# GpSimd makes the edges' one-hot rows, and the landmark loop's products and block copies are dealt out anew

## The chip, the cores and the metric

One core of a Trainium2 chip runs the whole program in one launch. The metric is the device time in microseconds, the median of several executions. For the kernel before they are 2507.85, 2507.54 and 2505.82 us, the median 2507.54.

## The reference, cut to what matters

The program is a "macaron" block over 32 x 256 rows of 128 values: an int8-quantised product, a Nystrom attention with a graph part, the quantised product again, a mixture of eight experts, a small attention, and the experts again, each behind a layer norm and added to the rows. The change touches two pieces of the first attention:

```python
# edges: 16384 of them, rows and columns in 0..1023, values drawn
contrib = adj_vals * data[adj_rows, adj_cols]
A_raw = jax.ops.segment_sum(contrib, adj_rows, num_segments=n)   # n = 256 here
# landmarks: means of 8 rows of q and k, 8 heads of 64, 32 landmarks, 32 batches
q_l = q.reshape(b, h, m, l, dh).mean(axis=3)
k_l = k.reshape(b, h, m, l, dh).mean(axis=3)
attn2 = jax.nn.softmax(jnp.einsum('bhid,bhjd->bhij', q_l, k_l), axis=-1)
attn2_inv = moore_penrose_pinv(attn2, 6)   # scale: max row sum times max column sum over everything
```

The kernel turns the edge list into a dense 256 x 256 matrix `Wadj`, whose product with the scores is summed along its rows.

## The kernel before, in words

Everything is written by hand: each engine has one instruction stream, and semaphores order them. `S[name]` is a semaphore, `wait_ge` waits for its value, `then_inc` raises it, `hold` is a wait with a count behind it.

**The group steps** (about 30 to 284 us of the profile). The rows are worked in eight groups of 1024 (`NG` = 8): layer norm (L332 to L362), quantised product (L413 to L438, L446 on GpSimd, L455 and L465 on TensorE), layer norm again, and the landmark means (L483 on VectorE, L489 on TensorE). Between these pieces each engine has a share of the edges, 16 tiles of 128 edges a group (`EG` = 16, 128 tiles in all). For one tile VectorE makes three rows of 256 bf16 values for each of the 128 edges: `EK` (L1708, one at the edge's column), `ER` (L1710, one at the edge's row) and `EV[0]` (L1712, the high part of the value at the column). ScalarE makes `EV[1]` and `EV[2]` out of EK and the value's two lower parts (L1721, two a tile). TensorE adds six products of 128x256 to PSUM (L1433), ER as the stationary side, EV as the moving one. Eight slots (`DEEP`) are in use; a slot is free when the products of the tile eight before are done (`ed_mm`). The order in which tiles and the other pieces follow one another is written out by hand in `first_dve`, `first_act` and `first_pe`; GpSimd has only `q_pool` (L446) once a group and `early_pool` (L1414 in the first group, L1417 in the sixth). `early_pe` puts parts of batch 0's attention (L1381 to L1393) between the products of groups 1 to 5.

**The landmark loop** (284 to 316 us) has four passes c, one for each pair of heads. In `b_pe` TensorE makes the pair's keys of all landmarks (L1458, into `H[2:4]`), then its queries (L1466, into `H[0:2]`), then 16 small products of query and key landmarks (L1476, into `TRq` and `Yq`; 32 records). VectorE copies the keys out (`KL`, L1757, L1758), ScalarE the queries (`QL`, L1618, L1619); there is one buffer of each, so both wait for the pass's small products. Then VectorE copies four 32x256 blocks out of TRq (L1763) and ScalarE four out of Yq (L1622) to `S2`. VectorE waits for all eight, takes the row maximum (L1736) and subtracts it (L1737); ScalarE takes the exponential (L1625); VectorE sums, inverts and multiplies (L1741 to L1743, `normal`) one pass later. After the loop the column sums of the four passes are made by TensorE (L1482) and their maxima by VectorE (`column`, L1751); `total` (L1747) takes the row sums. GpSimd makes the largest of them over all partitions (L1677), which scales the start of the inverse. SP moves blocks of S2 to `XB` (L2485) as soon as a pass is normalised, XB is transposed (L1504) and copied (L1627); then six passes of the inverse follow (L1558 to L1577).

After that the rounds run until 2514 us: experts (L876, L908), small attention, routing. The change has nothing in them.

Of the kernel before, what the change touches and what calls it, by code (L numbers as in the profile page):

```python
# [8 lines left out]
ALU = mybir.AluOpType  # L9
# [17 lines left out]
DEEP = 8  # L27
# [64 lines left out]
def build(nc, ins, out):  # L92
    ctx = ExitStack()
    with ctx:
# [1331 lines left out]
        def edges_pe(pe, g, lo, hi):  # L1426
            for j in range(lo, hi):
                q = j % DEEP
                pe.wait_ge(S["ed_v"], 3 * EG * g + 3 * (j + 1))
                pe.wait_ge(S["ed_a"], 2 * EG * g + 2 * (j + 1))  # L1430
                for u in range(2):
                    for k in range(3):
                        mm = pe.matmul(H[:, u, 0:SEQ], ER[:, q, u * P:(u + 1) * P], EV[:, q, k, :],  # L1433
                                       start=False, stop=False)
                mm.then_inc(S["ed_mm"], 1)
# [16 lines left out]
        def b_pe(pe):  # L1452
            pe.wait_ge(S["lm_cp"], LEAD + NG)
            for c in range(4):
# [5 lines left out]
                mm.then_inc(S["b_l"], 1)  # L1460
                if c >= 1:
# [6 lines left out]
                mm.then_inc(S["b_l"], 1)  # L1468
                pe.wait_ge(S["b_ql"], c + 1)
                pe.wait_ge(S["b_kl"], c + 1)  # L1470
                if c >= 1:
                    pe.wait_ge(S["b_s2d"], 4 * c)
                    pe.wait_ge(S["b_s2a"], 4 * c)
# [13 lines left out]
            pe.wait_ge(S["b_s2a"], 16)  # L1487
# [5 lines left out]
            pe.wait_ge(S["b_s2d"], 16)  # L1493
# [119 lines left out]
        def b_act(act):  # L1613
            for c in range(4):
# [5 lines left out]
                act.wait_ge(S["b_s"], c + 1)  # L1620
                for i in range(4):
# [80 lines left out]
        def edges_dve(dve, g, lo, hi):  # L1702

            for j in range(lo, hi):
# [5 lines left out]
                dve.tensor_scalar(ER[:, q, :], iota, erf[:, bass.ds(col, 1)], None,  # L1710
                                  ALU.is_equal).then_inc(S["ed_v"], 1)
                dve.tensor_scalar(EV[:, q, 0, :], iota, ecf[:, bass.ds(col, 1)], evh[:, bass.ds(col, 1)],  # L1712
                                  ALU.is_equal, ALU.mult).then_inc(S["ed_v"], 1)

        def edges_act(act, g, lo, hi):

            for j in range(lo, hi):
                q = j % DEEP
                hold(act, S["ed_v"], 3 * EG * g + 3 * j + 1)
# [4 lines left out]
        def b_dve(dve):  # L1724
# [8 lines left out]
            def shift(c):  # L1733
                dve.wait_ge(S["b_s2a"], 4 * (c + 1))
                dve.wait_ge(S["b_s2d"], 4 * (c + 1))
# [17 lines left out]
            for c in range(4):  # L1753
# [8 lines left out]
                for i in range(4):  # L1762
# [3 lines left out]
                if c >= 1:  # L1766
                    total(c - 1)
            column(0)
            column(1)
            normal(3)  # L1770
# [720 lines left out]
        def _(pool):  # L2491
# [60 lines left out]
            for p in range(2):  # L2552
# [9 lines left out]
                             tmp[:, 2, :].rearrange("p (g d) -> p d g", g=AH)).then_inc(S["w_pm"], 1)  # L2562
            for g in range(NG):
                q_pool(pool, g, FIRST_Q)
                early_pool(pool, g)
            b_pool(pool)
# [179 lines left out]
```

## Time and profile before

| | |
|---|---|
| median of three executions | 2507.54 us |
| the profiled execution, timed | 2515.66 us |
| its span, first to last instruction | 2513.9 us |
| TensorE products, weight loads | 2036.8 us, 1594.7 us busy |
| VectorE, ScalarE, GpSimd | 1426.1, 1236.0, 648.7 us busy |
| mean granted TensorE clock | 0.909 |

The page gives busy times, the chain of work that ended last (followed back from the last instruction), and groups of instructions by line, with the idle time of the engine before them and who ended it. A timeline row has start, duration, engine, line, operation, what it writes and reads with shapes, and the count merged into the row; in brackets stands the engine's idle time before it and the releaser as the profile infers it. A merged row's duration runs to the end of its last instruction. DVE is VectorE, ACT is ScalarE, POOL is GpSimd, PE and PEld are TensorE's products and weight loads. Float products of 32 bits show two records each.

### The profile page before, as it was taken

To read this page: it belongs to the slowest core of one execution; us is meant where nothing else is said; L and a number is where in the kernel's file an instruction comes from. 1 tells how busy PE (TensorE), PEld (TensorE's weight loads), DVE (VectorE), ACT (ScalarE), POOL (GpSimd) and SP (SyncE) were. 2 spreads that over 40 slices of the span, in tenths; PEclk is the share of its full clock that TensorE was granted. 3 is DMA by queue.
4 is the path that set the end of the run, shared out by engine and by line. 5 is a ranking of instruction groups with operands and counts; after the bars stand their busy time and mean duration, and the time that the engine had idled before them with its cause. 6 is when DMAs were issued, how large, how long until landed. Compare 5 with 4: busy or idle time off the path is not lost.

```text
span 2513.9 us, 38918 instructions
## 1 busy us (share of the span) xinstructions
PE 2036.8 (81%) x13610; PEld 1594.7 (63%) x13610; DVE 1426.1 (57%) x4130; ACT 1236.0 (49%) x2670; POOL 648.7 (26%) x663
## 2 busy tenths in 40 slices
PE   2766773587878888998899889989998999788884
PEld 1555552476557556875787578757875886665764
DVE  5877536453556675566556565666566356356522
ACT  3766413444446455555555564555455446335431
POOL 3111003333131133124223322332233124013052
PEclk9777885699889899999899999999999999899997
DMA  7100000112211211312132213221322312312121
GB/s 237 43 1 1 1 1 0 31 45 64 56 47 44 65 52 57 85 55 55 52 91 57 65 39 89 62 65 32 92 67 60 88 52 68 89 29 61 41 62 47
DMA packets 228948, 141.29 MB, mean 56 GB/s; under 512 B 116489, under 2 KB 206732, under 8 KB 228754
## 3 DMA queue, kind: packets, MB, share of 16 engines
q1 hardware_dynamic: 174320, 85.60, 13.4%
q0 software_dynamic: 16960, 34.74, 4.6%
q10 hardware_dynamic: 37474, 18.46, 2.6%
q8 instruction: 110, 1.80, 0.3%
q14 instruction: 84, 0.69, 0.1%
HBM read 82.48 MB, written 57.16 MB: 56 GB/s over the span
## 4 chain that ended last, share of the span: by engine, by line
PE 53%; DVE 24%; ACT 12%; issue 6%; DMA 2%; POOL 2%; SPq 1%; ACTq 0%; POOLq 0%; DVEq 0%
PE PS L908 17%; PE PS L876 9%; DVE AR L1085 3%; PE PS L1207 3%; PE PS L1170 3%; PE PS L1188 3%; PE PS L1433 2%; PE PS L1193 2%; ACT AR L1141 2%; DVE small L332 2%; ACT AR L837 2%; ACT AR L362 2%; DVE AR L795 2%; DVE xnT L1269 1%; PE PS L911 1%
## 5 line engine op out<-in xcount | busy, mean ns | idle before, releaser
L908 PE MATMUL PS<-AR,W 128*128 128x256 f32 x2560 | 653.0, 404 | 20.9 <-DVE AR L795 15.0
L795 DVE TENSOR_TENSOR AR<-AR,PS 128x512 f32<-128x512 f32 (+1 forms) x384 | 228.6, 597 | 653.9 <-ACT AR L837 525.8
L908 PEld LDWEIGHTS PS<-AR,W 128*128 128x128 f32 x2560 | 499.8, 204 | 92.1 <-issue 17.0
L837 ACT ACTIVATE AR<-PS 128x512 f32<-128x512 f32 (+1 forms) x384 | 201.1, 525 | 556.5 <-PE PS L908 439.1
L1085 DVE TENSOR_REDUCE AR<-PS 128x2 f32<-128x512 f32 x512 | 337.2, 688 | 160.0 <-PE PS L1170 155.6
L1141 ACT ACTIVATE AR<-PS 128x512 f32<-128x512 f32 x512 | 303.6, 600 | 236.3 <-PE PS L1193 231.9
L876 PE MATMUL PS<-AR,WO 128*128 128x256 f32 (+1 forms) x1536 | 357.7, 383 | 0.0
L876 PEld LDWEIGHTS PS<-AR,WO 128*128 128x128 f32 (+1 forms) x1536 | 295.5, 193 | 42.8
L1170 PE MATMUL PS<-AR 128*128 128x256 bf16 x1024 | 204.8, 287 | 40.4 <-DVE AR L1085 25.9
L743 POOL DMA_INDIRECT AR<-YE,gidx1c x128 | 128.8, 1007 | 379.8 <-issue 231.4
L743 POOL DMA_INDIRECT AR<-YE,gidx x128 | 128.3, 1002 | 350.9 <-ACT AR L1141 310.8
L1188 PE MATMUL PS<-AR 128*128 128x256 bf16 x1024 | 204.5, 282 | 13.3 <-ACT AR L1141 11.2
L726 POOL DMA_INDIRECT XE<-AR,sidx x128 | 130.6, 1020 | 274.8 <-DVE AR L795 142.8
L1193 PE MATMUL PS<-AR,pick 128*128 128x256 bf16 x1024 | 201.1, 279 | 0.0
L1433 PE MATMUL PS<-AR 128*128 128x256 bf16 x768 | 127.3, 333 | 81.6 <-ACT AR L1721 35.0
L726 POOL DMA_INDIRECT XE<-xn,sidx x128 | 126.8, 991 | 225.1 <-ACT AR L1141 135.7
L1170 PEld LDWEIGHTS PS<-AR 128*128 128x128 bf16 x1024 | 99.4, 119 | 103.7 <-DVE AR L1085 55.1
L1433 PEld LDWEIGHTS PS<-AR 128*128 128x128 bf16 x768 | 87.5, 118 | 116.9 <-DVE AR L1712 58.1
L1207 PE MATMUL PS<-AR 128*32 128x256 f32 x2048 | 141.6, 395 | 8.1 <-ACT AR L1141 8.1
L1188 PEld LDWEIGHTS PS<-AR 128*128 128x128 bf16 x1024 | 103.6, 117 | 49.7 <-ACT AR L1141 42.5
L1721 ACT ACTIVATE AR<-AR 128x256 bf16<-128x256 bf16 x256 | 107.5, 496 | 19.8 <-DVE AR L1708 17.0
L362 ACT ACTIVATE AR<-X,small 128x128 f32<-128x128 f32 x248 | 102.3, 489 | 13.6 <-DVE small L347 13.1
(359 smaller groups left out, 2771.5 us busy)
## 6 DMA issues: line engine op xcount, KB each, us to landing
AR<-XE SPq DMA_DIRECT2D x128, 128.0 KB, 2.1
YE<-AR ACTq DMA_DIRECT2D x128, 128.0 KB
AR<-QD SPq DMA_DIRECT2D x384, 32.0 KB
QD<-AR SPq DMA_DIRECT2D x8, 768.0 KB, 5.2
AR<-KD SPq DMA_DIRECT2D x64, 96.0 KB
W<-in_L_ffn_w_kernel_dram SPq DMA_DIRECT2D x2, 2560.0 KB, 13.5
OD<-AR SPq DMA_DIRECT2D x128, 36.0 KB
X<-in_L_attn_dense_dram SPq DMA_DIRECT2D x8, 512.0 KB, 4.5
```

What stands on the lines that cost most here:

```text
L726: pool.indirect_dma_start(rows_of(p, g), bass.IndirectOffsetOnAxis(ap=sidx[tab][:, k, t:t + 1], axis=0), rows[:, t, :], None, bounds_check ...
L743: pool.indirect_dma_start(yg[:, k, t, :], None, results_of(p, g), bass.IndirectOffsetOnAxis(ap=at[:, k, t:t + 1], axis=0), bounds_check=E ...
L795: ins = dve.tensor_tensor(hf[:, cols], gl[i % 2][:, cols], H[:, 2 * (i % 2) + 1, cols], ALU.mult)
L837: ins = act.activation(gl[i % 2][:, cols], H[:, 2 * (i % 2), cols], ACT.Gelu_apprx_tanh)
L876: mm = pe.matmul(Y[:, 0, 0:CAP], WO[rows, e, b, :], hid[e % 2][rows, b, :], start=(b == 0), stop=(b == HBLK - 1))
L908: mm = pe.matmul(H[:, b0, b * CAP:(b + 1) * CAP], w0[:, e, hb * P:(hb + 1) * P], xeT[e % 2], start=True, stop=True)
L1085: dve.tensor_reduce(mx[c % 2][:, :, b], score_bank(c, b).rearrange("p (h q) -> p h q", h=2), AX.X, ALU.max).then_inc(S["a_mx"], 1)
L1141: act.activation(EX[:, li, :], H[:, 2 + i % 2, :], ACT.Exp, scale=A_SCALE).then_inc(S["a_ex"], 1)
L1170: mm = pe.matmul(score_bank(c, b)[:, h * 256:(h + 1) * 256], keys(c, P, h, b), queries(c, b), start=True, stop=True)
L1188: pe.matmul(o[:, h * 256:(h + 1) * 256], keys(c, P, h, b), queries(c, b), start=(h == 0), stop=False, skip_group_check=True)
L1193: mm = pe.matmul(o.rearrange("p (h q t) -> p q h t", h=2, q=2)[:, q], pick[:, q * PB + b:q * PB + b + 1].broadcast_to([P, P]), MP[c % 2].r ...
L1433: mm = pe.matmul(H[:, u, 0:SEQ], ER[:, q, u * P:(u + 1) * P], EV[:, q, k, :], start=False, stop=False)
```

## The change

The row ER is made by GpSimd, in a new function `edges_pool`, with a semaphore of its own (`ed_r`); its 16 tiles a group are put around `q_pool` and `early_pool`. TensorE waits for `ed_r` too, and VectorE's count `ed_v` goes up by two a tile. In `b_pe` the key products of pass c+1 are issued between the query products and the small products of pass c. Of the eight block copies of a pass VectorE makes two and ScalarE six. After the loop `normal(3)` stands ahead of `column(0)` and `column(1)`.

```diff
@@ -1426,7 +1426,8 @@
         def edges_pe(pe, g, lo, hi):
             for j in range(lo, hi):
                 q = j % DEEP
-                pe.wait_ge(S["ed_v"], 3 * EG * g + 3 * (j + 1))
+                pe.wait_ge(S["ed_v"], 2 * EG * g + 2 * (j + 1))
+                pe.wait_ge(S["ed_r"], EG * g + j + 1)
                 pe.wait_ge(S["ed_a"], 2 * EG * g + 2 * (j + 1))
                 for u in range(2):
                     for k in range(3):
@@ -1451,13 +1452,17 @@
 
         def b_pe(pe):
             pe.wait_ge(S["lm_cp"], LEAD + NG)
-            for c in range(4):
+
+            def landmark_keys(c):
                 if c >= 1:
                     pe.wait_ge(S["b_kl"], c)
                 for a in range(2):
                     mm = pe.matmul(H[:, 2 + a, :], wqkv[:, 512 + c * P:512 + (c + 1) * P],
                                    mT[:, a * 512:(a + 1) * 512], start=True, stop=True)
                 mm.then_inc(S["b_l"], 1)
+
+            landmark_keys(0)
+            for c in range(4):
                 if c >= 1:
                     pe.wait_ge(S["b_ql"], c)
                 else:
@@ -1466,11 +1471,13 @@
                     mm = pe.matmul(H[:, a, :], wqkv[:, c * P:(c + 1) * P], mT[:, a * 512:(a + 1) * 512],
                                    start=True, stop=True)
                 mm.then_inc(S["b_l"], 1)
+                if c < 3:
+                    landmark_keys(c + 1)
                 pe.wait_ge(S["b_ql"], c + 1)
                 pe.wait_ge(S["b_kl"], c + 1)
                 if c >= 1:
-                    pe.wait_ge(S["b_s2d"], 4 * c)
-                    pe.wait_ge(S["b_s2a"], 4 * c)
+                    pe.wait_ge(S["b_s2d"], 2 * c)
+                    pe.wait_ge(S["b_s2a"], 6 * c)
                 for q in range(8):
                     for j in range(2):
                         mm = pe.matmul((TRq, Yq)[j][:, q, :], QL[64 * j:64 * j + 64, q * P:(q + 1) * P],
@@ -1484,13 +1491,13 @@
 
             for a in range(3):
                 column(a)
-            pe.wait_ge(S["b_s2a"], 16)
+            pe.wait_ge(S["b_s2a"], 24)
             for c in range(4):
                 for j in range(2):
                     mm = pe.matmul(Y[32 * c:32 * c + 32, j, 0:SEQ], ql0[64 * j:64 * j + 64, c, :],
                                    kT0[64 * j:64 * j + 64, c, :], start=True, stop=True, skip_group_check=True)
             mm.then_inc(B("a3")[0], 1)
-            pe.wait_ge(S["b_s2d"], 16)
+            pe.wait_ge(S["b_s2d"], 8)
             for u in range(2):
                 for c in range(4):
                     for j in range(2):
@@ -1618,6 +1625,9 @@
                 act.mul(QL, flat2(H[:, 0:2, :]), DH ** -0.5)
                 act.mul(ql0[:, c, :], H[:, 0, 0:LM], DH ** -0.5).then_inc(S["b_ql"], 1)
                 act.wait_ge(S["b_s"], c + 1)
+                for i in range(2, 4):
+                    act.copy(S2[32 * i:32 * i + 32, 2 * c, :, :],
+                             TRq[32 * i:32 * i + 32, :, 32 * i:32 * i + 32]).then_inc(S["b_s2a"], 1)
                 for i in range(4):
                     act.copy(S2[32 * i:32 * i + 32, 2 * c + 1, :, :],
                              Yq[32 * i:32 * i + 32, :, 32 * i:32 * i + 32]).then_inc(S["b_s2a"], 1)
@@ -1707,16 +1717,21 @@
                 col = EG * g + j
                 dve.tensor_scalar(EK[:, q, :], iota, ecf[:, bass.ds(col, 1)], None,
                                   ALU.is_equal).then_inc(S["ed_v"], 1)
-                dve.tensor_scalar(ER[:, q, :], iota, erf[:, bass.ds(col, 1)], None,
-                                  ALU.is_equal).then_inc(S["ed_v"], 1)
                 dve.tensor_scalar(EV[:, q, 0, :], iota, ecf[:, bass.ds(col, 1)], evh[:, bass.ds(col, 1)],
                                   ALU.is_equal, ALU.mult).then_inc(S["ed_v"], 1)
 
+        def edges_pool(pool, g, lo, hi):
+
+            for j in range(lo, hi):
+                hold(pool, S["ed_mm"], EG * g + j + 1)
+                pool.tensor_scalar(ER[:, j % DEEP, :], iota, erf[:, bass.ds(EG * g + j, 1)], None,
+                                   ALU.is_equal).then_inc(S["ed_r"], 1)
+
         def edges_act(act, g, lo, hi):
 
             for j in range(lo, hi):
                 q = j % DEEP
-                hold(act, S["ed_v"], 3 * EG * g + 3 * j + 1)
+                hold(act, S["ed_v"], 2 * EG * g + 2 * j + 1)
                 for k, v in ((1, evm), (2, evl)):
                     act.activation(EV[:, q, k, :], EK[:, q, :], ACT.Copy,
                                    scale=v[:, bass.ds(EG * g + j, 1)]).then_inc(S["ed_a"], 1)
@@ -1731,8 +1746,8 @@
                 return v[:, 16 * c:16 * c + 16]
 
             def shift(c):
-                dve.wait_ge(S["b_s2a"], 4 * (c + 1))
-                dve.wait_ge(S["b_s2d"], 4 * (c + 1))
+                dve.wait_ge(S["b_s2a"], 6 * (c + 1))
+                dve.wait_ge(S["b_s2d"], 2 * (c + 1))
                 ch.link(dve.tensor_reduce(of(mx2, c), seg(c), AX.X, ALU.max))
                 dve.tensor_tensor(seg(c), seg(c), bc(of(mx2, c), 16, LM), ALU.subtract).then_inc(S["b_sh"], 1)
 
@@ -1759,15 +1774,15 @@
                 if c >= 1:
                     normal(c - 1)
                 dve.wait_ge(S["b_s"], c + 1)
-                for i in range(4):
+                for i in range(2):
                     dve.tensor_copy(S2[32 * i:32 * i + 32, 2 * c, :, :],
                                     TRq[32 * i:32 * i + 32, :, 32 * i:32 * i + 32]).then_inc(S["b_s2d"], 1)
                 shift(c)
                 if c >= 1:
                     total(c - 1)
+            normal(3)
             column(0)
             column(1)
-            normal(3)
             column(2)
             total(3)
             column(3)
@@ -2560,9 +2575,13 @@
 
             pool.tensor_copy(tmp[:, 7, :].rearrange("p (d g) -> p d g", g=AH),
                              tmp[:, 2, :].rearrange("p (g d) -> p d g", g=AH)).then_inc(S["w_pm"], 1)
+            pool.wait_ge(S["ed_prep"], 1)
             for g in range(NG):
+                edges_pool(pool, g, 0, 4)
                 q_pool(pool, g, FIRST_Q)
+                edges_pool(pool, g, 4, 12)
                 early_pool(pool, g)
+                edges_pool(pool, g, 12, EG)
             b_pool(pool)
             round_pool(pool)
 
```

## Rows read from the trace of the kernel before

**Rows 1.** The page's chain that ended last, share of the span by engine.

```profile
PE 53%; DVE 24%; ACT 12%; issue 6%; DMA 2%; POOL 2%; SPq 1%; ACTq 0%; POOLq 0%; DVEq 0%
```

**Rows 2.** Windows by stage: length, busy PE, PEld, DVE, ACT, POOL, granted clock, DMA.

```profile
30.00:284.00 254.00, 169.61 (x1103) 127.56 (x1104) 188.86 (x786) 165.30 (x406) 33.05 (x10) 0.78 0.15 45
...
284.00:303.40 19.40, 14.88 (x89) 7.88 (x89) 12.69 (x24) 8.78 (x17) 0.68 (x2) 1.00 0.01 1
```

**Rows 3.** Groups by line and shape, 0 to 620 us: busy us, mean ns, idle.

```profile
L1721 ACT ACTIVATE AR<-AR 128x256 bf16<-128x256 bf16 x256 | 107.5, 496 | 19.8 <-DVE AR L1708 17.0 <-DVE AR L1710 2.6
...
L446 POOL TENSOR_SCALAR xnT<-tmp 128x1024 bf16<-128x1024 f32 x8 | 29.6, 3696 | 162.0 <-DVE tmp L417 162.0
```

**Rows 4.** Timeline of ScalarE in the fifth group, from the root on.

```profile
154.28 0.30 ACT L356 ACTIVATE small<-small,epsc 128x8 f32<-128x8 f32 x1 [1.23 <-DVE small L342]
...
156.00 0.91 ACT L1721 ACTIVATE AR<-AR 128x256 bf16<-128x256 bf16 x2 [0.51 <-DVE AR L1710]
...
156.81 3.17 ACT L362 ACTIVATE AR<-X,small 128x128 f32<-128x128 f32 x8
...
159.89 3.28 ACT L1721 ACTIVATE AR<-AR 128x256 bf16<-128x256 bf16 x8
```

**Rows 5.** Timeline of TensorE in the fifth group, tile 2 and early products.

```profile
160.92 1.44 PE L1433 MATMUL PS<-AR 128*128 128x256 bf16 x6 [2.12 <-DVE AR L1710]
...
164.40 3.26 PE L1389 MATMUL PS<-AR 128*128 128x512 f32 x4
```

**Rows 6.** Timeline of VectorE and GpSimd where both work.

```profile
152.11 3.67 POOL L446 TENSOR_SCALAR xnT<-tmp 128x1024 bf16<-128x1024 f32 x1 [27.08 <-DVE tmp L417]
...
153.51 0.17 DVE L337 TENSOR_TENSOR small<-small 128x8 f32<-128x8 f32 x1
...
154.36 0.28 DVE L1710 TENSOR_SCALAR AR<-AR 128x256 bf16<-128x256 bf16 x1
...
154.56 0.34 DVE L1712 TENSOR_SCALAR AR<-AR 128x256 bf16<-128x256 bf16 x1
...
154.81 1.05 DVE L1708 TENSOR_SCALAR AR<-AR 128x256 bf16<-128x256 bf16 x1
...
170.39 1.23 DVE L438 TENSOR_TENSOR X<-X,tmp 128x1024 f32<-128x1024 f32 x1
...
199.87 2.35 POOL L1417 TENSOR_TENSOR AR<-AR,wvb 128x1024 f32<-128x1024 f32 x1 [13.06 <-ACT AR L1406]
...
201.28 2.02 DVE L438 TENSOR_TENSOR X<-X,tmp 128x1024 f32<-128x1024 f32 x1
```

**Rows 7.** Windows of TensorE: length, busy, clock, around a long gap.

```profile
171.20:175.50 4.30, 0.00 (x0) 0.81 0.00 0
...
175.50:184.00 8.50, 6.49 (x30) 0.50 0.00 1
```

**Rows 8.** Timeline of the landmark passes c = 0 to 2.

```profile
288.70 2.06 PE L1476 MATMUL PS<-AR 64*128 64x128 f32 x32 [1.20 <-ACT AR L1619]
...
295.27 0.18 DVE L1758 COPY AR<-PS 128x32 f32<-128x32 f32 x1
...
295.95 2.06 PE L1476 MATMUL PS<-AR 64*128 64x128 f32 x32 [1.56 <-ACT AR L1619]
...
297.94 1.98 PE L1458 MATMUL PS<-AR 128*128 128x512 f32 x4
...
298.06 1.53 ACT L1622 COPY AR<-PS 32x256 f32<-32x256 f32 x4 [2.15 <-PE PS L1476]
...
298.06 1.77 DVE L1763 COPY AR<-PS 32x256 f32<-32x256 f32 x4 [1.00 <-PE PS L1476]
...
303.11 0.18 DVE L1758 COPY AR<-PS 128x32 f32<-128x32 f32 x1
...
303.39 2.06 PE L1476 MATMUL PS<-AR 64*128 64x128 f32 x32 [1.75 <-ACT AR L1619]
```

**Rows 9.** Timeline: GpSimd's reduction ahead of the inverse.

```profile
322.29 0.35 POOL L1677 PARTITION_ALL_REDUCE AR<-AR  x1 [31.62 <-DVE AR L1776]
```

## The prediction, made blind

> **What bounds the kernel now.** I read the chain that ended last first [rows 1]: the products of the later rounds (L908, L876) carry it, and the change does not touch them. Its whole text lies in two stretches ahead of the rounds, so I asked for these as windows [rows 2]: the eight group steps with the edges (30 to 284 us), and the start of the landmark stage. In the first no engine is full (TensorE 170 of 254 us, VectorE 189, ScalarE 165, GpSimd 33) and the granted clock is 0.78 of full; in the second it is full. So the question in both is which wait ends last, and I took the timeline of one group step (150 to 182 us; six of the eight look alike) and of one landmark pass.
>
> In the group step ScalarE's root of the next layer norm stands idle 1.23 us for VectorE's statistics, and later 0.51 us for an edge row of VectorE [rows 4]. Then come eight normalised rows (3.17 us) and edge tile 2 (0.91 us a tile for its two rows), and TensorE's product of tile 2 starts at 160.92 after 2.12 us of idle time [rows 4, 5]: the view names L1710, but ScalarE's tile 2 started at 159.89, so it is ScalarE that comes last. Behind that product follow turn, products, update, statistics, root: the loop that sets the step's length. In the landmark pass the loop is: small products L1476, block copies, maximum, subtraction, exponential, QL, next L1476.
>
> **Part 1: 128 edge rows ER leave VectorE.** Each costs VectorE 0.20 us from start to start (154.36 to 154.56 in [rows 6]), 1.6 us in the eight tiles between the statistics and the next root, 3.2 us a group. It is worth only what stands still for it. At the root it is at most the 1.23 us, beside it the 0.51 us, and TensorE's gap bounds both: tile 2 can't start before the landmark copy is out, its EK made, and ScalarE's 0.91 us done, about 1.4 us before 160.92. Working the six groups through in the same manner gives 0.2, 1.0, 1.2, 1.65, 1.8 and 2.25 us (the last three with a smaller gap at tile 0 too), together 8.1 us; first and last group nothing. A second gain could follow: behind the 2.1 us gap TensorE went to half clock and the four 512-column products took 3.26 us [rows 5], where the same shape takes 1.98 at full clock [rows 8]. A shorter gap may spare that, 1.3 to 2 us in up to three groups, so 6 us. The edge stage gains between 0 and 14 us if nothing else changes.
>
> **GpSimd's price.** The trace has no such row there. Nearest is L446, 3.70 us for 1024 columns with two operations [rows 3], so 0.9 us for 256; sixteen make 15 us and L446 3.7, in a step of 31: GpSimd keeps up. It runs eight slots ahead of TensorE, whose own new wait so costs nothing by this count; queued behind GpSimd's waits is L446, which may start under 1 us later than now, but its readers come 6 us after its end. The cover goes if an ER takes over 1.6 us.
>
> **What it does to VectorE** decides this part. During L446 (152.11 to 155.78) three edge rows pass at 0.28 to 0.34 us, and the fourth takes 1.05 instead of 0.28 [rows 6]; all eight L446 show one such stall of 0.77 us. And the update L438, 1.23 us alone, takes 2.02 beside GpSimd's L1417 [rows 6]. So two engines do stop each other in pieces of about 0.8 us, not for a whole instruction. An ER of 0.9 us may hold VectorE for 0 to 0.77 us. Placing the sixteen by the products that free their slots: ER 13 to 15 fall on the update, two on tiles 8 to 15, one or two on L417 and on tiles 2 to 5. Bounds: no stall, or 0.77 us on the update in eight groups (6 us) with the 8 us gain gone and up to 1 us a group behind tiles 2 to 5: +14 us. I take the middle, as the one L446 row stalls about a fifth of its length: half of the 8.1 lost (gain 4), 0.39 x 8 = 3.1 on the update, 1 us of clock won: **-1.9 us, bounds -14 and +14**.
>
> A rule bears on this. In the Trainium skill, page SBUF — State Buffer, section Who interferes with whom, the shared port pair is a lock held by whichever started first for its whole instruction, against VectorE operations in a two-port mode or with two SBUF inputs. The trace agrees on the kind (L1708, L438), not on the length: L337, with two SBUF inputs, took its usual 0.17 us inside L446, and three edge rows passed [rows 6]. By that rule a tile would cost VectorE much more; it is the third rival.
>
> **Part 2: key products ahead of the small ones.** TensorE now does key(c+1) between query(c) and small(c). Four records at 0.43 us make 1.73 us ([rows 8], L1458: 1.98 with the tail). It waits for VectorE's KL copy, which small(c) needs too, so for c = 1 and 2 it simply goes between. c = 0: TensorE is free at 287.50 (288.70 less 1.20), key(1) ends 289.25 instead of 288.70: +0.55. c = 1: the KL copies end 295.45, key(2) ends 297.2 instead of 295.95: +1.25. c = 2: 303.29, so 305.05 instead of 303.39: +1.65. c = 3 has none. What it takes away, key before the next query, was done while VectorE and ScalarE worked, and nobody waited for it: gain 0. Sum **+3.5 us**.
>
> **Part 3: block copies 4+4 become 2+6.** Both engines start together; four take VectorE 1.77 us, ScalarE 1.53 [rows 8]. Six on ScalarE take 0.36 + 5 x 0.39 = 2.3 us, and the maximum waits for all: +0.54 each, four times **+2.2 us**. VectorE's two saved copies only lengthen its wait. The table load of the first exponential stays under it.
>
> **Part 4: normal(3) before two column maxima.** The XB rows leave 1.2 us sooner, but the inverse's start also waits for GpSimd's reduction at 322.29 [rows 9], which follows all of VectorE's maxima and sums; these are the same work in another order, with 0.1 us less idle: **-0.1 us**.
>
> **The clock in part 2 and 3.** TensorE's gaps in this loop are now 1.2 to 1.75 us and the clock stays full [rows 2, 8]. After the change they are 3.4 to 4.1 us (from the end of query(c+1), 1.7 us after small(c), to the next KL copy, 5.8 us after it). In the edge stage gaps of 4.3 us end at half clock: 171.2 to 175.5 averages 0.81, then 0.50 for 8.5 us [rows 7]; from 80 us on the stage has seven gaps of over 4 us, and each ends or is followed at once by half clock. If it falls here, key and small (1.73 + 2.06) double twice, small once more: bounds 0 and +9.7. I take **+4**, since a fall late in the gap doubles only part. The inverse behind already runs its first two passes at half clock; it may gain or lose one pass, about 2 us, left in the range.
>
> Sum: -1.9 + 3.5 + 2.2 - 0.1 + 4.0 = **+7.7 us**. The profiled execution spans 2513.9 us (2515.66 timed), so its like would span 2521.6. It is 8 us above the median of the runs; I carry the difference over: 2507.5 + 7.7 = **2515.2 us**.
>
> **Rivals.** *A, ends faster:* GpSimd's ER meets VectorE hardly ever or for a few tenths, and the shorter gaps keep TensorE's clock up in the edge stage. Price -14, landmark +5.6 with no fall: -8.4, 2499 us. It decides when the edge stage wins over 10.6 us. For it: sixteen short rows against VectorE's idle 6 us plus 3.2 a step. Against: it needs all gains at once. *B, no change:* edge stage about -2, the landmark passes longer but at full clock: +3.7, 2511 us. *C, lock for the whole ER:* 0.92 instead of 0.39 on the update (7.4 us), no gain at the root, 1 to 2 rows behind tiles 2 to 5 (7 us), with +9.6 in the landmark stage: +24, 2532 us. Against: the rows that passed inside L446. *D, the change doesn't do what it says:* ER could be late for TensorE if GpSimd needs over 1.6 us; then each tile follows GpSimd, far above C. I leave it under C.
>
> **Chances and range.** Forecast 0.37, B 0.27, A 0.23, C (with D) 0.13. About 0.2% (5 us) is what a measurement of this kernel can tell from no change: slower 0.50, same 0.27, faster 0.23. The likeliest case alone has 2510 to 2520. The range reaches through A's price by 1 us, and into C until under 2 in 10 are out: 2498 to 2528.
>
> **What would show it.** In the landmark stage small products start 8.5 to 9.5 us apart instead of 7.3 to 7.4, with a key product right ahead; ScalarE has six copies of about 2.3 us. The granted clock of 290 to 320 tells the 4 us. In the edge stage: L1708's rows with a mean above 0.31 us or L438 above 1.3 speak for contention; ScalarE's idle before its root should vanish; GpSimd's row should be 0.5 to 1.0 us. I am wrong if the small products come no later, or if the edge stage shrinks by over 10 us.

## The result, and the profile after

The kernel before took 2508.9 us (median of 22 runs), the changed one 2518.7 us (22 runs). The ratio is 1.0043, with a 95% interval of 1.0029 to 1.0057: slower by about 10 us, 0.4%. The forecast was +7.7 us, the median of before carried with it 2515.2 us, the range 2498 to 2528.

The page of after, its first line, the busy time of each engine and the chain that ended last (before's shares are [rows 1]):

```profile
span 2526.2 us, 39046 instructions
...
PE 2043.0 (81%) x13610; PEld 1596.7 (63%) x13610; DVE 1407.3 (56%) x3994; ACT 1237.8 (49%) x2678; POOL 773.6 (31%) x791
...
PE 51%; DVE 23%; ACT 12%; issue 6%; DMA 3%; POOL 2%; SPq 1%; ACTq 0%; POOLq 0%; DVEq 0%
```

The page alone tells little: GpSimd's work has grown, the chain is the same. The places have to be read. First the landmark stage, which answers to [rows 8]. Timeline of after: start, duration, engine, line, operation, tiles, count, and in brackets the idle time before it. L1460 is the key product, L1483 the small one, L1629 and L1632 are ScalarE's copies, L1778 VectorE's.

```profile
295.56 2.06 PE L1483 MATMUL PS<-AR 64*128 64x128 f32 x32
...
302.81 3.35 PE L1460 MATMUL PS<-AR 128*128 128x512 f32 x4 [3.28 <-DVE AR L1773]
306.09 2.33 PE L1483 MATMUL PS<-AR 64*128 64x128 f32 x32
308.47 0.75 ACT L1629 COPY AR<-PS 32x256 f32<-32x256 f32 x2 [5.27 <-PE PS L1483]
308.47 0.86 DVE L1778 COPY AR<-PS 32x256 f32<-32x256 f32 x2 [4.11 <-PE PS L1483]
309.25 1.52 ACT L1632 COPY AR<-PS 32x256 f32<-32x256 f32 x4
310.81 0.69 DVE L1751 TENSOR_REDUCE AR<-AR 128x16 f32<-128x512 f32 x1 [1.47 <-ACT AR L1632]
...
314.22 3.78 PE L1460 MATMUL PS<-AR 128*128 128x512 f32 x4 [3.89 <-DVE AR L1773]
317.93 3.19 PE L1483 MATMUL PS<-AR 64*128 64x128 f32 x32
...
326.97 3.63 PE L1483 MATMUL PS<-AR 64*128 64x128 f32 x32 [3.93 <-DVE AR L1773]
```

Small products start 10.53, 11.84 and 9.04 us apart; before, 7.25 and 7.44, and the prediction had 8.5 to 9.5. In each of the middle passes a key product of 3.4 to 3.8 us stands right ahead of the small one, where the same shape took 1.98 us [rows 8]. VectorE is done with its two copies at 309.33 and stands 1.47 us for ScalarE's six. The windows of the same stretch (length, busy PE, PEld, DVE, ACT, POOL, granted clock, DMA share) show where the long records come from:

```profile
290.20:302.80 12.60, 9.32 (x48) 4.69 (x48) 5.48 (x10) 5.91 (x11) 0.68 (x2) 1.00 0.00 0
302.80:321.20 18.40, 14.50 (x77) 8.10 (x78) 7.18 (x14) 4.35 (x12) 0.00 (x0) 0.72 0.01 2
321.20:330.60 9.40, 5.47 (x37) 3.97 (x37) 5.64 (x10) 3.90 (x9) 0.00 (x0) 0.82 0.01 1
```

Up to 302.80 the clock is at its upper level, 2.4 GHz; behind the gap of 3.28 us it has fallen towards the lower one, 1.2 GHz.

Now the edge stage. Groups by line and shape of after, 30 to 285 us: busy us, mean ns of one, idle before them. L1718 is EK, L1720 EV, L337 the first statistics row.

```profile
L1720 DVE TENSOR_SCALAR AR<-AR 128x256 bf16<-128x256 bf16 x128 | 51.0, 399 | 0.0
L1718 DVE TENSOR_SCALAR AR<-AR 128x256 bf16<-128x256 bf16 x128 | 38.2, 299 | 1.2
...
L417 DVE TENSOR_SCALAR tmp<-AR,small 128x128 f32<-128x128 f32 x64 | 14.7, 304 | 0.3
L438 DVE TENSOR_TENSOR X<-X,tmp 128x1024 f32<-128x1024 f32 x8 | 12.0, 1497 | 0.3
...
L337 DVE TENSOR_TENSOR small<-small 128x8 f32<-128x8 f32 x15 | 6.1, 409 | 0.5
```

and the same view of before:

```profile
L1712 DVE TENSOR_SCALAR AR<-AR 128x256 bf16<-128x256 bf16 x128 | 45.6, 356 | 0.0
...
L417 DVE TENSOR_SCALAR tmp<-AR,small 128x128 f32<-128x128 f32 x64 | 13.3, 282 | 0.3
L438 DVE TENSOR_TENSOR X<-X,tmp 128x1024 f32<-128x1024 f32 x8 | 10.6, 1325 | 0.3
```

VectorE has 39.9 us of rows less, and of the kinds that are left several take longer: EV by 43 ns, L417 by 22, L438 by 172, L337 by 237 (172 before); EK does not (310 before). GpSimd's own row, which the trace of before did not have, has a mean of 0.99 us (0 to 620 us):

```profile
L1727 POOL TENSOR_SCALAR AR<-AR 128x256 bf16<-128x256 bf16 x128 | 125.5, 993 | 81.5 <-PE PS L1434 71.1 <-DVEq L1710 8.9
```

It stands 71.1 of its 81.5 idle us for slots that TensorE frees: GpSimd keeps up.

**Milestones.** I cut every trace at three instructions: the copy of the last group's landmark product (L483), behind which the landmark stage begins, GpSimd's reduction [rows 9] and VectorE's first quantising maximum (L413) of the rounds. Starts in us, and the length of the two stretches between:

| kernel | L483 | reduction | first L413 | landmark | inverse |
|---|---|---|---|---|---|
| before | 283.46 | 322.29 | 400.62 | 38.83 | 78.33 |
| after | 289.87 | 340.41 | 423.48 | 50.54 | 83.07 |
| landmark part only | 287.69 | 338.24 | 421.25 | 50.55 | 83.01 |
| edge part only | 285.19 | 323.95 | 402.25 | 38.76 | 78.30 |
| edge part again | 285.17 | 323.94 | 402.22 | 38.77 | 78.28 |
| keys only | 288.89 | 335.82 | 414.17 | 46.93 | 78.35 |
| copies only | 288.73 | 332.09 | 410.31 | 43.36 | 78.22 |
| after, gap filled | 287.17 | 331.56 | 414.26 | 44.39 | 82.70 |
| edges, own rows | 279.31 | 318.80 | 397.00 | 39.49 | 78.20 |
| before, own rows | 287.92 | 326.66 | 409.37 | 38.74 | 82.71 |
| before, idle GpSimd rows | 293.15 | 331.87 | 410.14 | 38.72 | 78.27 |
| two buffers | 287.74 | 322.14 | 404.84 | 34.40 | 82.70 |
| normal(3) first | 289.18 | 327.99 | 406.34 | 38.81 | 78.35 |
| both mended | 278.59 | 312.94 | 391.19 | 34.35 | 78.25 |

The landmark stretch repeats within 0.1 us with before's passes (38.72 to 38.83 in six traces; the seventh, edges with own rows, had 39.49, at a clock of 0.95 in its last 27 us where before has 0.97: its last two column products took 1.89 us, in the six 1.13 to 1.25), so there one trace decides a difference of a few us. The edge stage does not: with unchanged edge code it ended at 283.46, 287.69, 287.74, 288.73, 288.89 and 289.18, and with only L413's wait changed at 287.92; the mean of these seven is 287.7. The 6.4 us between before's and after's L483 are therefore mostly an early trace of before: with GpSimd's rows and the old wait of L413 the ends are 285.17, 285.19, 287.17 and 289.87, mean 286.9. And what follows, from L413 to the end of the span, took 2095 to 2113 us on the first chip, with the same code in all; a single profile says nothing on it.

The first chip ran before, after, and the two halves and two single edits of the first experiments. All other kernels ran on two other chips, where the kernel before itself took 2586 and 2590 us; each ratio below is to runs of before on the same chip.

### The profile page after: what moved, and what is told of

The parts are those of the page before. It is cut to its first block, busy times and chain, and to the rows that moved or that the text cites. A ratio compares the mean times of both kernels' runs of the same rounds, so it can differ in the third digit from the quotient of the medians.

```text
span 2526.2 us, 39046 instructions
## 1 busy us (share of the span) xinstructions
PE 2043.0 (81%) x13610; PEld 1596.7 (63%) x13610; DVE 1407.3 (56%) x3994; ACT 1237.8 (49%) x2678; POOL 773.6 (31%) x791
## 4 chain that ended last, share of the span: by engine, by line
PE 51%; DVE 23%; ACT 12%; issue 6%; DMA 3%; POOL 2%; SPq 1%; ACTq 0%; POOLq 0%; DVEq 0%
PE PS L908 16%; PE PS L876 8%; PE PS L1207 3%; DVE AR L1085 3%; PE PS L1170 3%; PE PS L1188 3%; PE PS L1193 2%; ACT AR L1141 2%; DVE small L332 2%; PE PS L1434 2%; ACT AR L362 2%; ACT AR L837 2%; DVE xnT L1269 1%; PE PS L911 1%; DVE AR L795 1%
## 5 line engine op out<-in xcount | busy, mean ns | idle before, releaser
L908 PE MATMUL PS<-AR,W 128*128 128x256 f32 x2560 | 642.4, 398 | 19.6 <-DVE AR L795 15.0
L908 PEld LDWEIGHTS PS<-AR,W 128*128 128x128 f32 x2560 | 490.6, 201 | 88.8 <-issue 17.0
L1188 PE MATMUL PS<-AR 128*128 128x256 bf16 x1024 | 204.3, 282 | 13.6 <-ACT AR L1141 11.4
L1727 POOL TENSOR_SCALAR AR<-AR 128x256 bf16<-128x256 bf16 x128 | 125.5, 993 | 81.5 <-PE PS L1434 71.1
```

The lines of the kernel that those rows point to most:

```text
L908: mm = pe.matmul(H[:, b0, b * CAP:(b + 1) * CAP], w0[:, e, hb * P:(hb + 1) * P], xeT[e % 2], start=True, stop=True)
L1188: pe.matmul(o[:, h * 256:(h + 1) * 256], keys(c, P, h, b), queries(c, b), start=(h == 0), stop=False, skip_group_check=True)
```

## The experiments

My theory: the landmark part makes the whole loss, as insertions at full clock (5.6 us) and by a fallen clock (the rest), and the edge part gives nothing, because what VectorE is spared is swallowed. The rival: the edge part costs, by GpSimd stopping VectorE.

**The landmark part alone.** All of the change in TensorE's, ScalarE's and VectorE's landmark code, edges as before.

```diff
+            landmark_keys(0)
+            for c in range(4):
...
+                if c < 3:
+                    landmark_keys(c + 1)
```

> The landmark part alone (key products ahead, copies 2 and 6, normal(3) first), the edges as before. My theory: in the changed kernel the stretch from the last landmark copy L483 to GpSimd's reduction grew from 38.8 to 50.5 us, so this kernel is slower than before by about 11 us less what the later stages may give back: +8 to +13 us in the times, the same rows in the trace (small products 10.5, 11.8 and 9.0 us apart), the edge stage as before (start of the landmark stage at 283.5 us). Rival, the edge stage did it: this kernel is within 4 us of before.

Measured: 1.0054 (1.0034 to 1.0075), as slow as after. Its landmark stretch is 50.55 us, after's within 0.01. Its edge stage ended at 287.69, not at 283.5: the first sign that this stage's end moves by itself.

**The edge part alone.**

```diff
-                dve.tensor_scalar(ER[:, q, :], iota, erf[:, bass.ds(col, 1)], None,
-                                  ALU.is_equal).then_inc(S["ed_v"], 1)
...
+                pool.tensor_scalar(ER[:, j % DEEP, :], iota, erf[:, bass.ds(EG * g + j, 1)], None,
+                                   ALU.is_equal).then_inc(S["ed_r"], 1)
```

> The edge rows on GpSimd alone, the landmark part as before. My theory: nothing of VectorE's saving reaches the path, since L413 waits for ScalarE's rows, and GpSimd's rows slow VectorE by about 0.7 us ahead of each root; with the clock's part the edge stage may end 0 to 7 us later (289.9 us in the changed kernel, 283.5 before). Times: 0 to +6 us. Rival from the prediction, the edge part gains by itself: the stage ends by 281 us and the times are 3 us or more below before. Rival, all of the loss is here: +9 us or more.

Measured: 1.0007 (0.9979 to 1.0034), and, the same kernel on another chip:

> The edge rows on GpSimd alone once more, beside the other kernels of this chip: the first time it was 0.07% above before with an interval of 0.6%. Theory: no gain and little loss, -3 to +4 us, L483 at 285 to 290 us, ScalarE's roots 11.6 us apart over the end of a group (11.1 before, 10.0 with the shorter wait). Rival: it is this part that costs, +6 us or more.

Measured: 0.9992 (0.9975 to 1.0009). Neither run tells the edge part from nothing; the narrower interval leaves it between 0.25% faster and 0.09% slower.

**One landmark edit at a time.** First landmark_keys alone, with four copies on each engine.

> Only the key products ahead of the small ones. By the count of the prediction the small products of passes 1 and 2 come 1.3 and 1.7 us later and those of pass 0 0.5 us: +3.5 us at full clock; the longer gaps let the clock fall, up to 6 us more. Theory: stretch from L483 to the reduction 45 to 49 us (38.8 before), times +5 to +9 us. Rival, no clock loss without the longer copies (gaps are 0.5 us shorter): +3.5 us, granted clock 1.00 until the last small products.

Measured: 1.0045 (1.0017 to 1.0074); landmark stretch +8.1 us. In its timeline (L1459 key, L1482 small product) the first long gap did nothing to the clock:

```profile
301.40 1.98 PE L1459 MATMUL PS<-AR 128*128 128x512 f32 x4 [2.85 <-DVE AR L1764]
303.31 2.06 PE L1482 MATMUL PS<-AR 64*128 64x128 f32 x32
```

The key products took 3.78 us only behind the next gap, of 3.43 us. Then the copies alone, keys in the old place:

```diff
-                for i in range(4):
+                for i in range(2):
                     dve.tensor_copy(S2[32 * i:32 * i + 32, 2 * c, :, :],
```

> Only the copies 2 and 6. Theory: each pass 0.5 us longer, the stretch from L483 to the reduction 40.8 to 41.2 us (38.8 before), clock full, since the gap grows only from 1.75 to 2.3 us; times +2 us, hardly told from no change. Rival: the gap of 2.3 us is already enough for the clock to fall, then +5 us or more.

Measured: 1.0011 (0.9990 to 1.0033); stretch +4.5 us where the copies' own 0.54 us make 2.2, so the theory's full clock did not hold. TensorE's timeline of that kernel (L1476 small products, second and third pass) shows the rest:

```profile
301.68 3.52 PE L1476 MATMUL PS<-AR 64*128 64x128 f32 x32 [2.02 <-ACT AR L1619]
...
311.04 2.72 PE L1476 MATMUL PS<-AR 64*128 64x128 f32 x32 [2.09 <-ACT AR L1619]
```

Behind gaps of 2.02 and 2.09 us the small products took 3.52 and 2.72 us instead of 2.06; before, behind 1.56 and 1.75 us, they took 2.06 [rows 8]. Beside the 2.85 us of keys only that left the clock full, the length of the gap alone does not decide; what does, no run here shows. The two edits are not additive (8.1 + 4.5 = 12.6 against 11.7 us), as one would expect where each of them alone already makes the clock fall.

**The gap filled.** After, with three 512-column products, whose result nobody reads, ahead of each later key product.

```diff
+                if c >= 1:
+                    pe.wait_ge(S["b_s2d"], 2 * c)
+                    pe.wait_ge(S["b_s2a"], 6 * c)
+                    for _ in range(3):
+                        pe.matmul(PS[:, 0, :], wqkv[:, 0:P], mT[:, 0:512], start=True, stop=True)
```

> The changed kernel with three unused 128x512 products of TensorE in each of the gaps of passes 1 to 3, after the block copies; their result is overwritten. Theory (the clock takes over half of the landmark loss): with the gap under 1.5 us the granted clock stays full, the small products take 2.06 us again and come 9.0, 9.5 and 8.0 us apart (10.5, 11.8, 9.0 in the changed kernel), the stretch from L483 to the reduction 43.5 to 45 us instead of 50.5; times 5 to 6 us below the changed kernel, so about +5 us against before. Rival: the products come late for another reason, and the stretch stays at 50 us or grows by the work added (2.6 us a pass).

Measured: 1.0038 (1.0013 to 1.0064), by time not told apart from after's 1.0043, so the 5 to 6 us that the times should have gained are not shown by them; the profiled execution had one of the long inverses (82.70 us). The trace is clear on the loop. Its timeline of TensorE (L1488 small products) and the window of the stage:

```profile
302.03 2.06 PE L1488 MATMUL PS<-AR 64*128 64x128 f32 x32
...
311.79 2.06 PE L1488 MATMUL PS<-AR 64*128 64x128 f32 x32
...
319.69 2.06 PE L1488 MATMUL PS<-AR 64*128 64x128 f32 x32 [0.54 <-ACT AR L1631]
```

```profile
287.50:330.00 42.50, 38.76 (x234) 19.80 (x234) 24.76 (x44) 16.96 (x37) 0.68 (x2) 0.97 0.01 2
```

Every small product is at 2.06 us, starts are 9.17, 9.76 and 7.90 us apart (the first stands at 292.86), the clock is 0.97. The stretch is 44.39 us: 5.56 over before, the insertions at full clock; the clock is the other 50.54 - 44.39 = 6.15 us. It can be counted in after's own rows too: the key products of 3.35 and 3.78 us and the small ones of 2.33, 3.19 and 3.63 are together 6.14 us over 1.98 and 2.06.

**The edge part with the wait mended.** Reading the group step of after showed what swallowed the gain (next section): L413 waits for eight normalised rows too many. Here it waits for its own.

```diff
-                dve.wait_ge(S["ln_xn"], TG * (l + 1))
+                own = where is FIRST_Q and (not isinstance(n, int) or n > 0)
+                dve.wait_ge(S["ln_xn"], TG * (l if own else l + 1))
```

> The edge rows on GpSimd, the landmark part as before, and the maximum L413 of the quantised product waits only for the rows of its own layer norm, no longer for the later ones of the group before. In the changed kernel L413 stood 0.94 us idle for those rows (186.19 us). Theory (VectorE's saving ends in that wait): L413 starts right behind the last edge tile, ScalarE's root of the next norm comes 0.9 us sooner in six groups, and the edge stage ends up to 5 us sooner than with GpSimd's rows alone (285.2 us), so 280 to 285 us; times 0 to -5 us against before. Rival: GpSimd's rows then fall on VectorE at other places, or TensorE's gaps only move, and nothing is gained.

Measured: 0.9969 (0.9947 to 0.9992), edge stage end 279.31, under the 280 to 285 of the theory. Groups by line, 30 to 285 us, of after and of this kernel show the wait go (the 3.3 us that stay are of the first group):

```profile
L413 DVE TENSOR_REDUCE small<-AR 128x8 f32<-128x1024 f32 x8 | 9.8, 1220 | 10.5 <-ACT xn L362 7.2 <-ACT AR L362 3.3
```

```profile
L414 DVE TENSOR_REDUCE small<-AR 128x8 f32<-128x1024 f32 x8 | 9.7, 1208 | 3.3 <-ACT AR L362 3.3
```

And the control, the same wait in the kernel before, where VectorE still has ER:

> The kernel before with the shorter wait of L413 alone, all rows ER on VectorE. It tells whether the gain of the kernel with GpSimd's rows and that wait was the wait alone. Theory: in the kernel before VectorE comes to L413 5.4 us after ScalarE's root and the rows it waits for are done 5.1 us after it, so the wait is 0 to 0.3 us and the times stay: within 3 us. Rival: the wait alone brings the 8 us.

Measured: 1.0005 (0.9991 to 1.0020), end 287.92: nothing. Only both together gain. The ratios of the two kernels with GpSimd's rows, 0.9992 and 0.9969, have intervals that still overlap; the ends of the stage do not: 279.31 here and 278.59 in the last experiment, against 285.17 at the earliest with the old wait.

**The contention by itself.** VectorE keeps its ER rows, and GpSimd makes the same 128 once more into a tile that nobody reads (each waits for the one four before it, and VectorE waits for the last before it copies the matrix out, behind the stage's end).

```diff
+                pool.tensor_scalar(spare[:, j % 4, :], iota, erf[:, bass.ds(EG * g + j, 1)], None,
+                                   ALU.is_equal).then_inc(S["ed_r"], 1)
```

> The kernel before, with GpSimd making the 128 edge rows a second time at the places of the changed kernel, into a spare tile that nobody reads; VectorE makes its own ER as before. So this is the contention alone, without the saving. Theory: VectorE's L1708, L1710 and L1712 rise from means of 310, 312 and 356 ns, L438 and L337 by some tenths; the edge stage is 3 to 8 us longer than with the same edge code alone (283.5 to 288.9 us in four traces) and the times +3 to +6 us. By the rule of a lock for the whole instruction each GpSimd row of 0.92 us stops an edge row for it: means of 500 ns or more and +15 us. Rival: no contention to speak of, times within 2 us.

Measured: 1.0036 (1.0015 to 1.0057), edge stage end 293.15, 5.5 us over the mean of 287.7 and 4.0 over the latest of the seven. Groups by line, 30 to 285 us:

```profile
L1712 DVE TENSOR_SCALAR AR<-AR 128x256 bf16<-128x256 bf16 x128 | 53.0, 414 | 0.0
L1710 DVE TENSOR_SCALAR AR<-AR 128x256 bf16<-128x256 bf16 x128 | 41.9, 328 | 0.0
...
L438 DVE TENSOR_TENSOR X<-X,tmp 128x1024 f32<-128x1024 f32 x8 | 11.8, 1478 | 0.3
```

The same kinds stretch as in after, from GpSimd's rows alone: EV by 58 ns, ER by 16, L438 by 153. So the contention is real, and no mean of the edge rows comes near the 500 ns of the rule of a lock.

**Two buffers.** The landmark part with a second KL and QL, so that keys c+1 are copied out while small(c) runs, and ScalarE takes query c+1 between its copies and the exponential. The edit also moves normal(c-1) behind VectorE's block copies in passes 1 and 2.

```diff
+        QLs, KLs = (QL, hk2[:, 0:NB * LM]), (KL, hk2[:, NB * LM:2 * NB * LM])
...
+                if c < 3:
+                    key_rows(c + 1)
```

> The landmark part of the change with two buffers each for KL and QL: VectorE copies the keys of pass c+1 while TensorE makes the small products of pass c, ScalarE copies the queries between its block copies and the exponential, and normal(c-1) fills VectorE's wait for ScalarE's copies. Edges as before. Theory: the keys ahead of the small products cost because of the single buffer; with two, the small products come 5.9 to 6.9 us apart (7.3 to 7.4 before), the clock stays full, the stretch from L483 to the reduction is 34 to 37 us (38.8 before) and the times are 0 to -5 us. Rival: VectorE's own work sets the pass and nothing is gained over before.

Measured: stretch 34.40 us, 4.43 under before and 16.1 under after; time 0.9993 (0.9972 to 1.0013). In its timeline the key copy L1774 runs beside the small product L1484:

```profile
299.05 2.06 PE L1484 MATMUL PS<-AR 64*128 64x128 f32 x32
299.32 1.22 DVE L1774 COPY AR<-PS 128x1024 f32<-128x1024 f32 x1
```

Starts of the small products are 5.6 us apart, under the 5.9 of the theory. But this trace's inverse took 82.70 us, not 78.3, which gives the 4.4 us back in this trace. How much of the gain is the second buffer and how much the new place of normal, no run tells.

**What makes the inverse long?** 82.7 to 83.1 us in after, landmark part only, gap filled and two buffers, 78.2 to 78.4 in the others by then. The first four have normal(3) ahead of the column maxima, the others don't, so I took that for the cause.

```diff
+            normal(3)
             column(0)
             column(1)
-            normal(3)
```

> Only normal(3) ahead of column(0) and column(1). In four traces with this order the first L413 of the rounds comes 82.7 to 83.1 us after GpSimd's reduction, in six without it 78.2 to 78.4, and TensorE's clock in the inverse rises 27 us after the reduction instead of 19. Theory: this order alone does it, through a gap of TensorE: stretch from L483 to the reduction 38.7 us as before, L413 82.5 to 83.2 us after the reduction, times +3 to +6 us. Rival: the late clock comes from the loop before, and the 78.3 us stay; times within 2 us.

Measured: 1.0004 (0.9981 to 1.0028), inverse 78.35 us. And "before, own rows", without that edit, had 82.71. The theory fell.

**Both mended.** Edges on GpSimd, L413's own rows, two buffers, normal(3) in its old place.

> Edge rows on GpSimd with L413 waiting only for its own rows, and the landmark part with two buffers each for KL and QL, the order of normal(3) as before the change. Theory: both parts of the change pay once the wait that swallowed them is gone: L483 at 278 to 282 us (279.3 with the first mend alone), stretch to the reduction 34 to 35 us (34.4 with the second), the first L413 of the rounds 78.3 us after the reduction; times 6 to 14 us below before. Rival: the clock takes it back in the rounds, no change.

Measured: 0.9936 (0.9910 to 0.9961), so 2570 us beside 2586: faster than before, and by the ratios than after. Edge stage end 278.59, stretch 34.35, inverse 78.25. By time that is 10 to 23 us, by the two stages of the trace 9.1 + 4.5 = 13.6 us (against the mean end of 287.7), at the upper edge of the 6 to 14 expected.

## Why the prediction was right, and where its steps were not

**Parts 2 and 3, at full clock: right.** Forecast 3.5 + 2.2 - 0.1 = 5.6 us, measured 5.56 with the gap filled. The starts of the small products came 9.17 and 9.76 us apart there, 1.9 and 2.3 us over before's; the prediction's terms for the same passes are 1.25 + 0.54 and 1.65 + 0.54. It rested on one reading: the key product was put ahead of a small one that waits for the same copy of KL, into the same single buffer, so it overlaps nothing new. Rival B, that these passes stay at full clock, fell.

**The clock in the landmark loop: right in kind, too small.** The forecast was +4 us, bounds 0 and 9.7; it was +6.15. I had let the fall come late in the gap. It did come late (key 3.35 us, small 2.33) in the second pass, but in the third the records are 3.78 and 3.19 and in the fourth 3.63, together about three quarters of a full double. That is why the small products of after start up to 11.8 us apart where I had 9.5 at most. I also took the fall as belonging to the keys' gaps of over 3.4 us; the copies alone, with 2.0 us, had one, and keys only had none behind 2.85 us.

**Part 1: the sum near, two of its steps wrong.** Forecast -1.9; the means of the ends give 286.9 - 287.7 = -0.8, the two timed runs +0.07% and -0.08%. With single ends spread over 5.7 us, -0.8 is no gain that can be told from none, and that the sum came near is luck: a gain counted at the roots that did not come, beside a price that was taken too high. The step that failed is "at the root it is at most the 1.23 us": I took the root to come earlier by whatever VectorE is spared. The sixth group of after:

```profile
181.09 0.30 ACT L356 ACTIVATE small<-small,epsc 128x8 f32<-128x8 f32 x1 [5.68 <-DVE small L342]
...
182.99 3.17 ACT L362 ACTIVATE xn<-X,small 128x128 f32<-128x128 f32 x8
...
184.19 0.53 DVE L1720 TENSOR_SCALAR AR<-AR 128x256 bf16<-128x256 bf16 x1
...
186.19 1.22 DVE L413 TENSOR_REDUCE small<-AR 128x8 f32<-128x1024 f32 x1 [0.94 <-ACT xn L362]
187.89 1.80 DVE L417 TENSOR_SCALAR tmp<-AR,small 128x128 f32<-128x128 f32 x8
191.03 3.63 POOL L446 TENSOR_SCALAR xnT<-tmp 128x1024 bf16<-128x1024 f32 x1
191.28 0.82 DVE L337 TENSOR_TENSOR small<-small 128x8 f32<-128x8 f32 x1
192.69 0.30 ACT L356 ACTIVATE small<-small,epsc 128x8 f32<-128x8 f32 x1 [1.75 <-DVE small L342]
```

VectorE reaches L413 early and stands there 0.94 us for ScalarE's rows L362, which end 182.99 + 3.17 = 186.16, 5.1 us after the root at 181.09. Before, VectorE's edge rows ran up to that maximum, 5.4 us after its root:

```profile
174.21 0.30 ACT L356 ACTIVATE small<-small,epsc 128x8 f32<-128x8 f32 x1 [5.41 <-DVE small L342]
...
179.60 1.21 DVE L413 TENSOR_REDUCE small<-AR 128x8 f32<-128x1024 f32 x1
...
185.31 0.30 ACT L356 ACTIVATE small<-small,epsc 128x8 f32<-128x8 f32 x1 [1.24 <-DVE small L342]
```

So only 5.4 - 5.1 = 0.3 us could be won there, of the 1.6 that VectorE was spared. The rows it waits for are not even its own: q_dve waits for TG * (l + 1) normalised rows, one norm more than it reads. Root to root was 11.1 us and became 11.6: -0.3 at the wait, +0.14 in L417, +0.65 in L337. This group is no exception. A trace has seven such pairs of roots; the first pair is 9.9 us apart in every trace, the other six are 11.08 to 11.11 us apart in before, and 11.60 to 11.84 in after and in the edge part alone. With the idle rows, where VectorE is spared nothing, the six are 11.60 to 11.84 too: here the saving brings next to nothing, and GpSimd's rows cost half a us. ScalarE's idle before the second root grew from 1.24 to 1.75 us, where I had said it should vanish. With the wait mended the same two roots stand 9.95 us apart:

```profile
175.67 0.30 ACT L356 ACTIVATE small<-small,epsc 128x8 f32<-128x8 f32 x1 [6.07 <-DVE small L342]
...
179.68 1.21 DVE L414 TENSOR_REDUCE small<-AR 128x8 f32<-128x1024 f32 x1
...
185.62 0.30 ACT L356 ACTIVATE small<-small,epsc 128x8 f32<-128x8 f32 x1
```

The maximum (L414 there) starts 4.0 us after the root and no idle time stands ahead of it or of the second root. The end of that stage, 279.31, is 8.4 us under 287.7 and the time 0.31% under before: as much as the 8.1 us that I had summed for the roots and tile 2. That the two figures meet is partly chance, since mine stood before GpSimd's price and the measured one behind it. The gain was there; a wait that I had not looked at was next.

The second step, GpSimd's price on VectorE, was about right in size and off in place. GpSimd's row is 0.99 us (estimate 0.9). On the update I had taken 0.39 us; it was 1497 - 1325 = 172 ns in the pair of views, and 0.24 us in the sixth group (177.00 in a fence below, 1.47 against 1.23 us [rows 6]). In exchange L337, which before passed inside L446 at 0.17 us [rows 6], takes 0.82 in five groups of after, as it now meets L446's start. In sum, by the kernel with idle rows, the contention is 5.5 us of the stage (one trace; by the time 0.36%, 3.9 to 14.8 us), where the forecast had 3.1 on the update and 4.05 at the roots, 7.2 us.

**Rival C, a lock for the whole ER, is out.** Rows of both engines around the update:

```profile
175.12 5.03 POOL L1727 TENSOR_SCALAR AR<-AR 128x256 bf16<-128x256 bf16 x5 [4.95 <-PE PS L1434]
...
177.00 1.47 DVE L438 TENSOR_TENSOR X<-X,tmp 128x1024 f32<-128x1024 f32 x1
...
184.07 1.10 POOL L1727 TENSOR_SCALAR AR<-AR 128x256 bf16<-128x256 bf16 x1 [3.92 <-PE PS L1434]
```

GpSimd runs five rows without a break from 175.12 to 180.15, and the update, which has two SBUF inputs, runs through the middle of them at 0.24 us over its undisturbed time. At 184.07 GpSimd starts a row of 1.10 us, and VectorE's EV at 184.19 takes 0.53 instead of 0.34. The Trainium skill, page SBUF — State Buffer, section Who interferes with whom, has the loser blocked for the winner's whole instruction; these rows agree that the two engines hold each other up and not that it lasts so long, and the measurement decides.

**Rival A, faster by full gains at once, was wrong for this change,** but its edge half came true once the wait was mended.

**The inverse: left open, and it is still.** I had said that it may gain or lose one pass, about 2 us. In five of fourteen traces it took 4.4 to 4.8 us longer. A window of before, 18 to 28 us after GpSimd's reduction, and the same of after:

```profile
340.30:350.30 10.00, 8.21 (x43) 5.51 (x41) 3.49 (x9) 1.65 (x5) 0.00 (x0) 0.96 0.00 0
```

```profile
358.40:368.40 10.00, 8.83 (x25) 5.75 (x25) 2.72 (x7) 1.24 (x3) 0.00 (x0) 0.51 0.00 0
```

Before is at 2.4 GHz for nearly all of it, with 43 products recorded; after is at 1.2 GHz, with 25. In windows of 2 us the clock rises 18 to 20 us after the reduction in before and 26 to 28 us after it in after; 8 to 9 us more at half the clock, with TensorE busy most of the time, make about 4 us (an estimate). So the clock's late rise goes with the 4.4 us and is of their size; why it comes late in some traces is not shown. It is not normal(3)'s place alone, and before with only L413's wait changed had it too. So how much of it belongs to this change can't be said: without it the change makes -0.8 + 11.7 = 10.9 us, with after's 4.7 it makes 15.6, and the timed ratio (7.3 to 14.3 us of 2508.9) is nearer the first. The +7.7 us of the forecast lies inside the timed interval; it held no such term, only room for it in the range.

## What to carry to other kernels

A product put earlier in an engine's order only helps if its result has a place to go: with one buffer it waits for the same copy as what it was put ahead of, and is a pure insertion; with a second buffer, and the copies and normal moved with it, +11.7 us became -4.4. Work taken off an engine pays only up to that engine's next wait, so read on from the wait that should go to the next one behind it, and look whether a cumulative count waits for more than it reads. And a stage where one trace repeats to 0.1 us may be judged from one trace; one that ends anywhere in 5.7 us may not.

## What the runs showed of the hardware

TensorE's clock fell behind gaps of only 2.0 us in a loop of short products (small product 3.52 us), while gaps of 1.56 and 1.75 us in the same loop, and one of 2.85 us with the key products ahead, left it at 2.4 GHz; three products that fill the gap, read by nobody, gave 6.15 us of the stage back. GpSimd's one-hot row of 256 columns takes 0.99 us where VectorE's takes 0.20 from start to start, and stretches VectorE's instructions beside it by 0.19 and 0.24 us in the rows shown, not by the row's length. The kernel before itself took 2509 us on one chip and 2586 and 2590 us on two others; that difference is eight times what the change makes, and no run here explains it.
